# Layer 1 of a two-layer transformer: where the distance bias is added and which engine sums the rope parts

## The reference

```
q = rope(x @ Wq); k = rope(x @ Wk); v = x @ Wv        # four heads share k and v
scores = q @ k.T                                      # per head, 256 x 256
scores = scores - slope[h] * |query - key|            # distance bias, slope[h] = 2 ** (-(h + 1) / 2)
scores = 30 * tanh(scores / sqrt(128) / 30)
scores = where(key <= query, scores, -inf)
out = softmax(scores) @ v, then @ Wo + bo
```

## Time and profile before

| what | us |
|---|---|
| median of 3 runs | 549.31 (547.53 to 551.34) |
| the profiled execution | 547.13 |
| its span, first to last instruction | 545.3 |

### The profile page before, as it was taken

One profiled execution on the slowest core, in us unless ns is written; L12 is line 12 of the kernel. 1 busy time (PEld: TensorE's weight loads), 2 busy tenths in 40 slices (PEclk: granted clock), 3 DMA queues, 4 the chain that ended last, 5 costly groups with the idle time before them and its releaser, 6 DMA issues.

```text
span 545.3 us, 10738 instructions
## 1 busy us (share of the span) xinstructions
PE 500.7 (92%) x3608; PEld 437.6 (80%) x3608; DVE 379.6 (70%) x820; ACT 338.2 (62%) x755; POOL 300.3 (55%) x293
## 2 busy tenths in 40 slices
PE   8888999999997899789993869999999999999995
PEld 7677888888885687568872768999999999999884
DVE  2679888888884136766563689778866996678646
ACT  5546777767767245534440687778776777676573
POOL 4846777777764115746561277667545654565320
PEclk9999999999999999799996989999999999999998
DMA  8939999920000562245585000000000000000001
GB/s 275 391 102 385 315 330 313 325 75 0 0 0 0 222 253 78 79 130 164 160 268 203 2 1 0 2 1 1 2 1 2 0 1 2 1 2 1 0 22 59
DMA packets 17598, 56.79 MB, mean 104 GB/s; under 512 B 2597, under 2 KB 12331, under 8 KB 15755
## 3 DMA queue, kind: packets, MB, share of 16 engines
q1 hardware_dynamic: 14800, 49.81, 26.9%
q0 software_dynamic: 2752, 6.40, 3.5%
HBM read 49.19 MB, written 28.45 MB: 142 GB/s over the span
## 4 chain that ended last, share of the span: by engine, by line
PE 65%; DVE 9%; issue 8%; POOL 7%; ACT 6%; DMA 3%; SPq 1%; POOLq 0%; DVEq 0%; ACTq 0%
PE bank L442 9%; PE bank L444 9%; PE bank L443 9%; PE bank L510 5%; POOL y_rows L2025 5%; PE bank L553 4%; PE bank L572 3%; PE bank L697 2%; PE bank L555 2%; PE bank L682 2%; PE bank L683 2%; PE bank L684 2%; PE bank L583 2%; DMA wqk_raw<-in_wqk 2%; PE bank L664 2%
## 5 line engine op out<-in xcount | busy, mean ns | idle before, releaser
L1056 ACT ACTIVATE probs<-bank,neg_max,q_scale 128x256 f32<-128x256 f32 (+1 forms) x128 | 63.7, 507 | 39.4 <-DVE neg_max L1677 39.4
L1890 POOL TENSOR_TENSOR probs<-probs,inv_sum 128x512 f32<-128x512 f32 x64 | 51.6, 826 | 43.9 <-DVE inv_sum L1685 43.9
L1923 POOL TENSOR_TENSOR exps<-exps,tables 128x256 f32<-128x256 f32 x32 | 24.5, 766 | 71.8 <-ACT exps L1163 71.6
L1910 POOL TENSOR_TENSOR swapped<-swapped,tables 128x512 f32<-128x512 f32 x32 | 43.4, 1359 | 25.8 <-ACT swapped L1087 25.6
L1163 ACT ACTIVATE exps<-bank 128x768 f32<-128x768 f32 x32 | 25.9, 809 | 41.2 <-PE bank L664 41.2
L1507 DVE TENSOR_TENSOR q_lo<-q_sum,q_hi 128x512 fp32r<-128x512 f32 x32 | 27.3, 854 | 29.5 <-ACT q_hi L1120 29.3
L1663 DVE TENSOR_TENSOR swapped<-bank,tables 32x512 f32<-32x512 f32 x64 | 44.4, 693 | 1.4
L1882 POOL TENSOR_TENSOR qT<-qT,swapped 128x512 f32<-128x512 f32 x32 | 40.8, 1275 | 7.1 <-DVE swapped L1663 7.1
L2025 POOL DMA_INDIRECT y_rows<-y_slot,dest x31 | 30.0, 968 | 25.1 <-issue 18.9
L442 PE MATMUL bank<-x,wq_hi 128*128 128x256 f32 x128 | 38.8, 303 | 4.9 <-DVE q_sum L1494 4.9
L553 PE MATMUL bank<-keysT,qT 128*128 128x256 f32 x128 | 38.3, 381 | 0.7 <-ACT wo_full L1283 0.7
(11 more groups left out here) (279 smaller groups left out, 1784.6 us busy)
## 6 DMA issues: line engine op xcount, KB each, us to landing
slots<-in_c_unused SPq DMA_DIRECT2D x20, 1036.0 KB, 36.5
gu_all<-in_gate_up SPq DMA_DIRECT2D x4, 1024.0 KB, 7.8
xg<-slots SPq DMA_DIRECT2D x31, 129.5 KB
wvo_raw<-in_wvo SPq DMA_DIRECT2D x1, 2560.0 KB, 19.9
dn_all<-in_down SPq DMA_DIRECT2D x1, 2048.0 KB, 8.1
wq_full<-in_Wq SPq DMA_DIRECT2D x1, 2048.0 KB, 15.8
wo_raw<-in_Wo SPq DMA_DIRECT2D x1, 2048.0 KB
yg<-y_rows SPq DMA_DIRECT2D x4, 512.0 KB, 5.2
```

What stands on the lines that cost most here:

```text
L1056: ins = act.activation(probs[:, par, h, c0:c1], bank[:, 2 * par + h, c0:c1], ACT.Exp, bias=neg_max[:, par, i:i + 1], scale=q_scale[:, b, t ...
L1890: ins = pool.tensor_tensor(some, some, inv, ALU.mult)
L1910: pool.tensor_tensor(sw, sw, sin_rows(), ALU.mult).then_inc(at1["sin_done"], 1)
```

## The change

The bias is no longer a product. A table `distance` (128 x 2 x 256 floats) holds minus slope times the distance of query and key for the first two heads. In every step VectorE takes the scores from their two banks, adds the table times 2 ** -(n mod 8), and writes `exps`; tanh then reads `exps` in place of the bank, and the next scores wait until VectorE has read the bank. The sum of the two query parts goes from VectorE to GpSimd, right behind the sine part. The bias tiles, their clearing and their two loads go; a smaller zero tile feeds the warm-up products, and the table is loaded by GpSimd's queue.

```diff
 # constants
+    distance = np.abs(pos[None, None, :] - pos[0:P, None, None]) * -slopes[None, 0:2, None]
-    alibi_keys = sb("alibi_keys", [P, T], BF16)
-    alibi_queries = sb("alibi_queries", [P, H, T], BF16)
+    zeros_bf = sb("zeros_bf", [P, T], BF16)
+    distance = sb("distance", [P, 2, T])
...
 # pe_scores1
         if n:
-            eng.wait_ge(at1["capped"], n)
+            eng.wait_ge(at1["biased"], n)
         for tile in range(2):
...
-            three_pass(eng, dst, k_hi[:, b % 2, p // 2, keys], k_lo[:, b % 2, p // 2, keys],
-                       q_hi[:, n % 4, :, queries], q_lo[:, n % 4, :, queries], True, False)
-            mm = eng.matmul(dst, alibi_keys[:, keys], alibi_queries[:, 2 * p:2 * p + 2, queries],
-                            start=False, stop=True, skip_group_check=True)
+            mm = three_pass(eng, dst, k_hi[:, b % 2, p // 2, keys], k_lo[:, b % 2, p // 2, keys],
+                            q_hi[:, n % 4, :, queries], q_lo[:, n % 4, :, queries], True, True)
...
 # act_layer1
-                act.wait_ge(at1["scores_done"], n + 1)
-                if n >= 2:
-                    act.wait_ge(at1["ctx_done"], n - 1)
-                act.activation(exps[:, n % 2, :], scores1, ACT.Tanh, scale=DQ ** -0.5 / 30.0).then_inc(at1["capped"], 1)
+                act.wait_ge(at1["biased"], n + 1)
+                act.activation(exps[:, n % 2, :], exps[:, n % 2, :], ACT.Tanh, scale=DQ ** -0.5 / 30.0).then_inc(at1["capped"], 1)
...
 # dve_layer1: query_sum and its four calls go (one for each of queries 0 to 2, one in the loop)
+        def add_bias(n):
+            slope = 2.0 ** -(n % PAIRS)
+            dve.wait_ge(at1["scores_done"], n + 1)
+            if n == 0:
+                dve.wait_ge(ld["alibi_in"], 32)
+            if n >= 2:
+                dve.wait_ge(at1["ctx_done"], n - 1)
+            dve.scalar_tensor_tensor(out=pair_view(exps[:, n % 2, 0:2 * T]), in0=distance[:], scalar=slope,
+                                     in1=pair_view(scores1[:, 0:2 * T]), op0=ALU.mult, op1=ALU.add)
+            dve.scalar_tensor_tensor(out=pair_view(exps[:, n % 2, 2 * T:3 * T]), in0=distance[:, :, 0:P], scalar=slope,
+                                     in1=pair_view(scores1[:, 2 * T:3 * T]), op0=ALU.mult,
+                                     op1=ALU.add).then_inc(at1["biased"], 1)
...
+            if b < B:
+                add_bias(n)
             if n + 2 < B * PAIRS:
                 query_lo(n + 2)
             if n + 3 < B * PAIRS:
                 query_cos(n + 3)
             if 1 <= n < B * PAIRS + 1:
                 context_norm(n - 1)
-            if n + 3 < B * PAIRS:
-                query_sum(n + 3)
             if n >= 2:
                 context_lo(n - 2)
...
 # pool_layer1
-        def sin_queries(m):
+        def turn_queries(m):
             pool.wait_ge(at1["swap_done"], m + 1)
             sw = pair_view(swapped[:, m % 2, :])
             pool.tensor_tensor(sw, sw, sin_rows(), ALU.mult).then_inc(at1["sin_done"], 1)
+            pool.wait_ge(at1["sin_done"], m + 1)
+            pool.wait_ge(at1["cos_done"], m + 1)
+            pool.tensor_tensor(q_sum[:, m % 2, :], q_sum[:, m % 2, :], swapped[:, m % 2, :],
+                               ALU.add).then_inc(at1["q_summed"], 1)
...
 # gpsimd, setup
-        pool.memset(alibi_keys[:], 0.0).then_inc(ld["cleared"], 1)
-        pool.memset(alibi_queries[:], 0.0).then_inc(ld["cleared"], 1)
+        pool.memset(zeros_bf[:], 0.0).then_inc(ld["cleared"], 1)
...
-        pool.wait_ge(ld["cleared"], 2)
-        pool.wait_ge(su["warmed"], 1)
-        pool.dma_start(alibi_queries[0:6], a["c_alibi_queries"]).then_inc(ld["alibi_in"], 16)
-        pool.dma_start(alibi_keys[0:6], a["c_alibi_keys"]).then_inc(ld["alibi_in"], 16)
+        pool.dma_start(distance[:], a["c_distance"].rearrange("p (h t) -> p h t", h=2)).then_inc(ld["alibi_in"], 16)
```

More of the change, by code:

```diff
@@ L98, in shape_constants @@
     triangles = np.concatenate([part[:, None] < part[None, :], np.ones((P, P))], 1)
-    out = dict(c_ident=np.eye(P, dtype=np.float32), c_mask=mask, c_alibi_keys=alibi_keys,
-               c_alibi_queries=alibi_queries, c_route=route, c_unused=unused, c_triangles=triangles,
+    out = dict(c_ident=np.eye(P, dtype=np.float32), c_mask=mask, c_distance=distance.reshape(P, 2 * T),
+               c_route=route, c_unused=unused, c_triangles=triangles,
                c_key_tables=np.concatenate([key_cos.reshape(P, 2 * ROPE), key_sin.reshape(P, 2 * ROPE)], 1),
@@ L293, in build @@
               "latents lat_done latT_hi_done latT_lo_done q_scaled keyT_done keysT_copied fold_done "
-              "fold_scaled fold_T_done fold_q_copied fold_o_done fold_o_copied rope_cols warmed")
+              "fold_scaled fold_T_done fold_q_copied fold_o_done fold_o_copied rope_cols")
     ln = sems("norm", "xT_done xT_hi_done xT_lo_done y_done y_read var_ready sqrt_done x_new")
@@ L308, in build @@
                "ctx_copied max_step max_ready probs_ready probsT_done probsT_copied")
-    at1 = sems("a1", "q_done swap_done cos_done sin_done q_summed q_hi q_ready scores_done capped masked exp_done "
+    at1 = sems("a1", "q_done biased swap_done cos_done sin_done q_summed q_hi q_ready scores_done capped masked exp_done "
                "ctx_done ctx_norm ctxT_done c_hi c_lo out_done")
@@ L481, in pe_logits @@
             if b == 1 and t == 0:
-                eng.wait_ge(ld["alibi_in"], 48)
+                eng.wait_ge(ld["alibi_in"], 32)
             eng.matmul(dst, ones_bf, marks[:, t:t + 1, :].broadcast_to([P, 2, E]), start=False, stop=False,
@@ L498, in keep_busy @@
         for i in range(n):
-            mm = pe.matmul(bank[:, 7, 0:T], alibi_keys[:, 0:P], alibi_keys[:], start=True, stop=True)
+            mm = pe.matmul(bank[:, 7, 0:T], zeros_bf[:, 0:P], zeros_bf[:], start=True, stop=True)
         return mm
@@ L878, in _ @@
         pe.wait_ge(ld["cleared"], 1)
-        keep_busy(pe, WARM[0]).then_inc(su["warmed"], 1)
+        keep_busy(pe, WARM[0])
         pe.wait_ge(su["wa_hi"], 1)
@@ L1495, in query_cos @@
                               ALU.mult).then_inc(at1["cos_done"], 1)
[L1497 to L1502, removed]
         def query_lo(m):
@@ L1537, in dve_layer1 @@
         query_cos(0)
-        query_sum(0)
         keys_lo(0, 0)
@@ L1934, in pool_layer1 @@
         for m in range(3):
-            sin_queries(m)
+            turn_queries(m)
         for n in range(B * PAIRS):
@@ L1943, in pool_layer1 @@
             if n + 3 < B * PAIRS:
-                sin_queries(n + 3)
+                turn_queries(n + 3)
             if 1 <= n <= PAIRS:
@@ L2001, in _ @@
         pool.memset(swapped[0:64], 0.0).then_inc(ld["cleared"], 1)
-        pool.wait_ge(ld["cleared"], 3)
+        pool.wait_ge(ld["cleared"], 2)
         pool.wait_ge(su["rope_cols"], 4)
```

2 lines of the change are left out of this document (removed).

## The result

The changed kernel takes **579.9 us** (median of 4 runs, 577.32 to 583.70) against 549.3 for the kernel before (547.53 to 551.34): 1.056 times as long, 95% interval 1.051 to 1.061. The profiled execution took 580.52 us, its span is 578.7.

What follows compares the result with a forecast made beforehand. Layer 1 was taken as bound by PE, 6.0 us a step. The profiled 547.1 us plus 33.0 (31.4 from first to last tanh, 1.6 for the first tanh, 0 for setup and tail) gave 580 us, range 560 to 596.

Steps and rivals of the forecast that it cites:

- the loop: In layer 1, tanh, masks, exp, context high half, low half, bias and next tanh close a circle: 5.9 us a step.
- the extras: VectorE's side work and waits between context low half and next bias lengthen the steps: 57.2 us in all.
- The start: The first tanh waits for VectorE's low half of query 1 and the bias: +1.6 us, between +0.8 and +2.4.
- Setup and tail at 0: Setup's altered loads and waits, and the tail behind the last tanh, were each to add 0 us.
- The stops: VectorE stands still during GpSimd passes, such as key low halves behind the new sum: seven stops at 0.6 us.
- the hop: Hand-over from VectorE's bias to ScalarE's tanh, counted in the 1.10 us taken for the two bias instructions.
- rival 4: VectorE's bias runs at half rate: 0.9 us a step more, 608 us; chance 0.02.
- rival 1: PE stays the bound, side work falling into VectorE's idle times: 537 us, or 540; chance 0.05.
- rival 2: Half of the extra time in layer 1's steps is hidden: some 552 us; chance 0.05.
- rival 3: PE's granted clock falls as it waits in every step: free at 0.94, 594 us at 0.75; chance 0.10.

Runs made afterwards that it cites:

- The two pads: The changed kernel with a 512-float memset on VectorE in steps 1 to 31, right ahead of the bias: 594.04 us; right behind it: 580.92 us.
- the reordered list: The changed kernel with VectorE's bias of the next step still behind the context low half but ahead of the side work: 554.16 us, ratio 1.003.
- the run with the setup alone: The kernel before plus the changed setup: table loaded but unused, separate zero tile, warm-up wait gone, bias products kept: 550.92 us, ratio 0.998.
- the kernel with both edits: The changed kernel with VectorE's context norm ahead of the cosine and ScalarE's context high half ahead of exp: 572.79 us, ratio 1.037.
- the list reordered and spread: The changed kernel with side work behind the bias, high half ahead of exp, norm ahead of cosine, expert tile and binarised weights spread: 546.01 us, ratio 0.988.
- the kernel with the sum back: The changed kernel with the sum of the query parts back on VectorE, between context norm and low half, the bias kept: 594.66 us.

## Why the prediction was right, point by point

**The time.** 580 was forecast and 579.9 measured, but two of its terms missed in opposite directions: first to last tanh was to grow by 31.4 and grew by 28.2; the first tanh was to come 1.6 later and came 5.2 later. That the figures agree to 0.1 us is luck: the forecast added 33.0 to the 547.1 of one profiled run, while the medians differ by 30.6. What holds is the loop and most of the extras, with an error of some 2 us in 31.

**The loop.** Right in place and length: 5.9 by rows, 5.85 in steps 7 and 23. That "nothing of it can run ahead" was right, but the circuit was read incompletely. I named the branch through masks and exp alone; the branch through swaps, cosine and norm is 0.16 us shorter (5.69), and in steps 4 and 6 GpSimd's masks, sine and sum make a third, which I had priced as an extra of 0.6. The number did not depend on that; the two edits that move the high half ahead of exp did, and they brought next to nothing.

**The extras.** The two pads and the reordered list show the mechanism: work between low half and bias is paid (0.48 us of a 0.485 us pad in most steps), and behind the bias it is not. Sizes, in us:

| step | forecast | measured |
|---|---|---|
| 8 | 9.4 | 10.96 |
| 9, 10 | 7.8, 7.1 | 7.96, 7.04 |
| 11, 13 | 8.5, 8.4 | 8.55, 8.42 |
| 12, 14 | 7.1 each | 6.93 each |
| 15 | 9.1 | 9.09 |
| 3, 5 | 9.7 each | 9.60, 9.61 |
| 0, 1, 2 | 8.7, 7.1, 7.0 | 8.35, 6.92, 6.84 |
| 4, 6, 7 | 7.7, 7.7, 7.2 | 6.91, 6.93, 5.85 |

By batch the extras over 5.85 are 14.2, 19.1, 15.3 and 6.7 (forecast 17.6, 17.3, 15.6, 6.7). Two places are off. In steps 4, 6 and 7 I added the output weights' halves (0.6 on ScalarE, and GpSimd's 1.3) to the loop. GpSimd in step 7 of the changed kernel:

```profile
373.12 1.74 POOL L1938 TENSOR_TENSOR wo_lo<-wo_raw,wo_hi 128x512 fp32r<-128x512 f32 x1
375.60 0.74 POOL L1914 TENSOR_TENSOR exps<-exps,tables 128x256 f32<-128x256 f32 x1 [0.75 <-ACT exps L1146]
...
381.29 1.18 POOL L1922 TENSOR_TENSOR x_rows<-x_rows,tables 128x512 f32<-128x512 f32 x1
382.43 1.18 POOL L1914 TENSOR_TENSOR exps<-exps,tables 128x256 f32<-128x256 f32 x1
```

The weights' low half ends at 374.86, before tanh (374.68 to 375.53) does: GpSimd still waits for tanh, so it is free. On ScalarE their high half (378.74 to 379.36) lies in the wait for the bias, and is free too. In step 8 the same queue is late. Its row add (L1922), behind sum and weights, runs past the end of tanh (380.53 + 0.85), the masks start at 382.43, 1.05 us after it (0.07 in step 7), and the four expert rows beside these passes take 3.2 us against 2.61 in the earlier trace rows; together the 1.6 that were missing:

```profile
386.31 3.22 DVE L1383 SCALAR_TENSOR_TENSOR x_rows<-yg,p_top,x_rows 128x256 f32<-128x256 f32 x4
```

For the key sums in steps 3, 5 and 13 I had counted GpSimd's queue; for step 8 I had not, although sum, weights and row add stand there one behind another.

**The start.** From the first sine product to the first tanh it takes 10.5 us for 8.6, so +1.9 for the forecast 1.6. The other 3.4 lie ahead of the layer, and the run with the setup alone shows them without any cost in the median. By medians the sum is 28.2 + 1.9 = 30.1 against 30.6 measured. Setup and tail at 0: right.

**The stops.** The forecast let the key low half wait for GpSimd's sum until 5.4 us after tanh. Step 22 of the changed kernel (its tanh starts at 495.70), GpSimd's sum and VectorE's key low half:

```profile
499.83 1.29 POOL L1900 TENSOR_TENSOR q_sum<-q_sum,swapped 128x512 f32<-128x512 f32 x1
500.51 1.16 DVE L1469 TENSOR_TENSOR k_lo<-k_sum,k_hi 128x512 fp32r<-128x512 f32 x1
```

The sum ends 501.12 - 495.70 = 5.42 after tanh, and the low half 0.55 behind it; in the step 22 of the kernel with both edits, above, it is 497.62 - 492.20 = 5.42 and the same 0.55. That agrees with the Trainium skill (SBUF — State Buffer, Who interferes with whom), by which a VectorE instruction with two SBUF inputs and a GpSimd one that reads SBUF exclude each other.

**The bias itself.** Forecast 1.10 with the hop. From 379.48 (step 7) to tanh at 380.53 it is 1.05. The wide one takes 0.60 from start to start (379.48 to 380.08), as the plain add in the earlier trace rows, the narrow one 0.41 against 0.42 in the earlier trace rows, so rival 4, the half rate, is out. The Trainium skill (Vector Engine (DVE) Microarchitecture Reference, Points that are easy to get wrong) makes that a rule for two SBUF sources that are not bf16. No run here has a bias of that kind, but the expert rows are the same instruction with both sources in SBUF: 0.45 to 0.48 us against 0.42 for a plain add, so they do not show it either.

**The other rivals.** PE stays the bound (rival 1): no, but with the list reordered and spread it is, at the 201.5 us named above. Half the extras hidden (rival 2): no. The clock (rival 3): 0.97 over the stretch of the earlier trace rows, and PE is not what is waited for, so it costs little. PE was to be busy near 80% in batch 1: it was 84% over the 54.60 us of that stretch, and 87% from the tanh of step 8 to that of step 16 (57.3 of 65.9 us), and why it is more stays open. And PE's idle time lies not where I put it, before context products and scores, but ahead of the query products, which wait for VectorE's cosine (18.5 us, in the waits above): scores of n+1 are done early, and PE then waits for the bank of the queries.

## What to carry to other kernels

Where a change puts an engine into a circle (here tanh, masks, high half, low half, bias), its price is the longest way round, and all that stands in that engine's list between the last link and the new one; so look for idle time behind the new link and put the side work there. Before cutting one branch of such a circle, time every other branch of the same step: here three closed it, two of them within 0.16 us in the same step, and cutting one alone gave next to nothing. A total that comes out right can hide two terms that are wrong with opposite signs, so compare it step by step.

## What the runs showed of the hardware

- VectorE's four expert rows (128 x 256, both sources in SBUF, L1383) took 4.52 us in step 8 of one kernel, beside back-to-back GpSimd passes, 2.27 us as side work of its step 16, where GpSimd passes ran beside part of them, and 1.78 us in step 8 of the kernel with the sum back, where GpSimd was idle: up to 2.5 times as long for the same work. The low halves and the sum show the same stretch: VectorE's sum took 1.69 us in a step of the kernel with the sum back, for 0.69 at its median in the earlier trace rows.
- The granted clock between 180 and 190 us, behind the setup and ahead of layer 1, was 1.00 in the profile before, 0.67 in that after, with PE busy 8.73 of the 10 us in both, and 0.56 to 1.00 in the others. The first tanh of single profiles came between 314.3 and 323.1 us; with the setup alone it came 5.3 us later than in the kernel before, and the medians of the two agree within 0.5%.
